# Scores of the last two cross-attentions from fp32r parts, with shared key places, keys' weights streamed in quarters, and values one step further ahead

## The reference

```python
def _cross_attention(q_in, kv_in, wq, bq, wk, bk, wv, bv, wo, bo, bias_k, bias_v):
    qh = (q_in @ wq + bq).reshape(b, q_len, H, K)
    kh = (kv_in @ wk + bk).reshape(b, t, H, K)
    vh = (kv_in @ wv + bv).reshape(b, t, H, K)
    kh = jnp.concatenate([kh, jnp.broadcast_to(bias_k, (b, 1, H, K))], axis=1)
    vh = jnp.concatenate([vh, jnp.broadcast_to(bias_v, (b, 1, H, K))], axis=1)
    logits = jnp.einsum('bqhk,bthk->bhqt', qh, kh) / jnp.sqrt(K)
    ctx = jnp.einsum('bhqt,bthk->bqhk', jax.nn.softmax(logits), vh).reshape(b, q_len, H * K)
    return ctx @ wo + bo
# x = x + attention 1(layer_norm(x)); x = x + attention 2(layer_norm(x)); x = x + mlp(layer_norm(x))
```

## Time and profile before

| | before |
|---|---|
| median of 3 runs | 1069.7 us (1068.66 to 1070.24) |
| the profiled execution, its own time | 1069.85 us |
| its span in the trace | 1068.0 us |
| PE, PEld busy share of the span | 94%, 74% |
| DVE, ACT, POOL busy share | 61%, 48%, 38% |
| mean granted TensorE clock | 0.992 |

### The profile page before, as it was taken

One profiled execution on the slowest core, in us unless ns is written; L12 is line 12 of the kernel. 1 busy time (PEld: TensorE's weight loads), 2 busy tenths in 40 slices (PEclk: granted clock), 3 DMA queues, 4 the chain that ended last, 5 costly groups with the idle time before them and its releaser, 6 DMA issues.

```text
span 1068.0 us, 18116 instructions
## 1 busy us (share of the span) xinstructions
PE 1006.1 (94%) x7252; PEld 789.6 (74%) x7252; DVE 656.5 (61%) x1119; ACT 512.2 (48%) x1026; POOL 402.8 (38%) x424
## 2 busy tenths in 40 slices
PE   6999999997998899999999999999999999989997
PEld 3667566555665898986777778777777877769997
DVE  4658999896787588355445436855434554554552
ACT  2557888876775554334333323323332332335552
POOL 2535689898876233002122113232211212443110
PEclk9999999999999899999999999999999999999999
DMA  9102000000000700020000114100000000200000
GB/s 322 61 1 80 1 1 1 2 1 2 2 1 2 256 2 2 1 79 1 2 1 1 29 52 158 56 24 1 1 1 1 2 1 1 79 1 12 20 21 30
DMA packets 17463, 34.90 MB, mean 33 GB/s; under 512 B 3554, under 2 KB 8420, under 8 KB 16740
## 3 DMA queue, kind: packets, MB, share of 16 engines
q1 hardware_dynamic: 17380, 33.75, 9.3%
HBM read 31.65 MB, written 2.10 MB: 32 GB/s over the span
## 4 chain that ended last, share of the span: by engine, by line
PE 74%; POOL 10%; ACT 6%; DVE 5%; issue 4%; DMA 0%; SPq 0%; POOLq 0%; DVEq 0%
PE work L938 11%; PE work L815 10%; PE scores L874 10%; PE work L891 5%; PE work L927 4%; POOL pair L1972 3%; PE work L674 3%; PE work L675 3%; PE work L676 3%; PE scores L674 3%; PE scores L676 3%; PE scores L675 3%; PE work L539 2%; PE work L601 2%; PE work L909 2%
## 5 line engine op out<-in xcount | busy, mean ns | idle before, releaser
L938 PE MATMUL work<-pair,probsT 128*128 128x256 f32 x512 | 120.5, 389 | 11.1 <-ACT pair L1845 8.9
L1931 POOL TENSOR_SCALAR stat<-stat 128x2 f32<-128x2 f32 (+1 forms) x49 | 11.2, 228 | 301.5 <-DVE stat L1060 300.3
L938 PEld LDWEIGHTS work<-pair,probsT 128*128 128x128 f32 x512 | 95.8, 192 | 35.4 <-issue 20.4
L815 PE MATMUL work<-ctxT,w 128*128 128x128 f32 x992 | 116.1, 275 | 1.8 <-ACT pair L1845 1.1
L815 PEld LDWEIGHTS work<-ctxT,w 128*128 128x128 f32 x992 | 114.5, 192 | 3.0 <-ACT pair L1845 1.3
L874 PE MATMUL scores<-pair,act_bufs 128*128 128x512 f32 x256 | 115.2, 592 | 0.0
L1836 ACT ACTIVATE pair<-work 128x512 f32<-128x512 f32 x64 | 38.2, 598 | 160.2 <-PE work L891 160.2
L1826 ACT ACTIVATE kvT<-work,cols 128x128 f32<-128x128 f32 x120 | 34.3, 369 | 142.1 <-PE work L815 142.1
L2086 POOL TENSOR_TENSOR probs<-probs,smax 128x1024 f32<-128x1024 f32 x22 | 42.0, 1909 | 152.6 <-DVE smax L1459 152.6
L1439 DVE TENSOR_REDUCE smax<-scores 128x16 f32<-128x1024 f32 x32 | 39.2, 1225 | 79.6 <-PE scores L874 79.6
L874 PEld LDWEIGHTS scores<-pair,act_bufs 128*128 128x128 f32 x256 | 46.3, 190 | 46.0 <-issue 45.9
(11 more groups left out here) (190 smaller groups left out, 2548.9 us busy)
## 6 DMA issues: line engine op xcount, KB each, us to landing
w<-in_l_wk SPq DMA_DIRECT2D x8, 512.0 KB, 7.2
w<-in_l_wq SPq DMA_DIRECT2D x8, 512.0 KB, 7.7
w<-in_l_wo SPq DMA_DIRECT2D x8, 512.0 KB, 8.1
w<-in_l_wv SPq DMA_DIRECT2D x8, 512.0 KB, 5.6
x<-in_x SPq DMA_DIRECT2D x1, 2048.0 KB, 13.7
out<-x SPq DMA_DIRECT2D x8, 256.0 KB, 2.1
pair<-in_xT SPq DMA_DIRECT2D x1, 1536.0 KB, 7.9
pair<-in_l_fc SPq DMA_DIRECT2D x1, 1024.0 KB, 5.1
```

The costliest lines, as they stand in the source:

```text
L815: last = mm(bank[:, h * P:(h + 1) * P], w[:, c, (4 * g + h) * K3:(4 * g + h + 1) * K3], ctxT[:, c, p * P:(p + 1) * P], start=(c == 0), sto ...
L938: last = mm(step_banks(j + 1)[0][:, 0:D], probsT_bufs[j % 2][:, q, :], pv[n % 2][:, bb, q, :], start=(q == 0), stop=(q == GH // 2 - 1))
```

## The change

1. `tile_scores` computes with `products`: for each of four key groups and two halves of the contraction, three fp32r matmuls of 256 columns (24 for a tile, in place of 4 fp32 ones of 512 columns). The tokens are kept as a high and a low part: DVE's `tile_source` writes both from PSUM (one instruction before, two now). The key products too: ACT copies the high part out, and DVE subtracts it from PSUM for the low part (`key_low`, two instructions a step). Whoever waited for ACT's copy of a key product (`a_pk`) now waits for DVE's low part (`d_kl`).
2. The key products lie in ten places, each of one group and one batch of the pair, given out by a table (`places_of_keys`); room for two comes from the half of `w3_wk` that is no longer used: the keys' weights are loaded one group at a time for every pair of batches (32 loads of 512 KB, two slots, in place of 8).
3. Values are worked on three steps ahead, not two.
4. ACT runs a one-column Gelu and a one-column Exp ahead of the first use of each; `key_bias(0)` and `key_bias(1)` go ahead of the stage's loop.
5. The last MLP's parts move to other addresses, and the copy of its first weight waits for the last value projection in place of an output.

```diff
         def value_of(j):
-            return j + 2 if 0 <= j + 2 < 8 * PAIRS else None
+            return j + 3 if 0 <= j + 3 < 8 * PAIRS else None
...
             for g in range(4):
-                load_w3(1, g, "kqo")
-
+                if g < 2:
+                    load_keys(g)
+                load_w3(1, g, "qo")
+
+            e.wait_ge(pe_f1, 4 * B)
+            for g in range(2):
+                load_w3(1, g, "v")
+            for i in range(2, 4):
+                e.wait_ge(pe_kp, i - 1)
+                load_keys(i)
...
             def first_free(j):
 
                 e.wait_ge(d_mr, B)
-                e.wait_ge(a_pk, 2 * keys_before(j))
+                e.wait_ge(d_kl, 2 * keys_before(j))
...
-                for half in range(2):
+                for g in range(4):
+                    k = place_at[PLACES[n, g][bb]]
                     for c in range(DC):
-                        last = mm(sc[j % 2][:, half * BANK:(half + 1) * BANK],
-                                  fixed[j // 2 % 2][:, c, t * P:(t + 1) * P],
-                                  pk[n % 2][:, bb, c, half * BANK:(half + 1) * BANK], start=(c == 0), stop=(c == DC - 1))
+                        last = products(sc[j % 2][:, g * QUARTER:(g + 1) * QUARTER],
+                                        [v[:, c, t * P:(t + 1) * P] for v in src_l3[j // 2 % 2]],
+                                        [all_keys[:, k + part, c, :] for part in range(2)], c == 0, c == DC - 1)
...
                     if q == 0:
                         third_free(j)
-                        e.wait_ge(a_pk, 2 * keys_before(j + 1) - 1)
+                        e.wait_ge(d_kl, 2 * keys_before(j + 1) - 1)
...
+            def key_low(i):
+
+                for c in range(DC):
+                    e.wait_ge(a_pk, 2 * i + c + 1)
+                    v.tensor_tensor(both_keys(i, c, 1), step_banks(i - 4)[2 + c][:, :].rearrange("p (h b k) -> p b h k", h=4, b=2),
+                                    both_keys(i, c, 0).bitcast(F32), ALU.subtract).then_inc(d_kl, 1)
...
+                if tile_of(j) is not None:
+                    tile_max_over(j)
+                if key_of(j) is not None:
+                    key_low(key_of(j))
                 if tile_of(j) is not None:
                     tile_shifted(j)
...
+            act(scratch[:, :], tanh_gate[:, :], ACT.Gelu_apprx_tanh)
...
+            key_bias(0)
+            key_bias(1)
+            act(scratch[:, :], tanh_gate[:, :], ACT.Exp)
             for j in STEPS:
                 key, value = key_of(j), value_of(j)
                 if key is not None:
-                    key_bias(key)
+                    if key >= 2:
+                        key_bias(key)
                     key_products(key)
```

More of the change, by code:

```diff
@@ L128, in build @@
         tanh_gate = sb("tanh_gate", [P, 1])
+        scratch = sb("scratch", [P, 1])
         probs_late = sb("probs_late", [P, GS + H3])
@@ L212, in parts_at @@
                     for i, k in enumerate(("high", "low"))]
+        src_l3 = [[nc.alloc_sbuf_tensor_at(f"src_l3_{i}_{k}", [P, DC, T], F32R, offset=at + 4 * i * DC * T)[:, :, :]
+                   for k, at in (("high", act_at), ("low", pair_at[1] + 4 * 2 * (n_kq + n_vo)))] for i in range(2)]
+        KEY_PLACES = 10
+        QUARTER = GS // 4
+        keys_at = w3_at + 4 * WN
+        all_keys = nc.alloc_sbuf_tensor_at("all_keys", [P, (pair_at[1] - keys_at) // 4 + n_kq * 2], F32R, offset=keys_at)
+        all_keys = all_keys[:, :].rearrange("p (k c n) -> p k c n", c=DC, n=QUARTER)
+        place_at = [(at - keys_at) // (4 * DC * QUARTER) + 2 * k for at, n in ((keys_at, 2), (pair_at[0], 4), (pair_at[1], 4))
+                    for k in range(n)]
+        assert len(place_at) == KEY_PLACES
         n_w, n_src, n_hid = 4 * DC * F, 4 * DC * T, 4 * FC * T
@@ L250, in build @@
         names += [f"l{i}_w{k}" for i in range(3) for k in "qkvo"]
-        names += [f"l3_w{k}_{g}" for k in "qkvo" for g in range(4)]
+        names += [f"l3_w{k}_{g}" for k in "qvo" for g in range(4)] + ["l3_wk_0", "l3_wk_1"]
         s_in = {n: sem(f"in_{n}") for n in names}
@@ L342, in key_bank, with places_of_keys, both_keys @@
             return fbank[i] if i < 2 else step_banks(i - 4)[0]
+        def places_of_keys():
+            places, used_until = {}, [-4 * PAIRS] * KEY_PLACES
+            for i in range(8 * PAIRS):
+                n, g = divmod(i, 4)
+                both = sorted(sorted(range(KEY_PLACES), key=lambda k: used_until[k])[:2])
+                assert max(used_until[k] for k in both) <= i - 4
+                places[n, g] = *both, max(0, *(used_until[k] + 1 for k in both))
+                for bb, k in enumerate(both):
+                    used_until[k] = 4 * n + 2 * bb + 1
+            return places
+        PLACES = places_of_keys()
+        def both_keys(i, c, part):
+            first, second, _ = PLACES[divmod(i, 4)]
+            a, b = place_at[first] + part, place_at[second] + part
+            return all_keys[:, a:b + 1:b - a, c, :].rearrange("p b (h k) -> p b h k", h=4)
         def attention_of(i):
@@ L409, in load_w3, with load_keys @@
                 heads, ks = slice(4 * g, 4 * g + 4), slice(4 * g * K3, (4 * g + 4) * K3)
[L410 to L412 removed]
+                for k in which:
                     src = A[f"l3_w{k}{a}"]
[L414 to L419 removed]
+                    if k == "v":
+                        load(f"l3_wv_{g}", w3_wv[:, g, :, :], src.rearrange("p (c n) -> p c n", c=DC)[:, :, ks])
+                    else:
+                        dst = w3_wq if k == "q" else w3_wo
+                        load(f"l3_w{k}_{g}", dst[:, heads, :], src.rearrange("p (h d) -> p h d", h=H3)[:, heads, :])
+            def load_keys(i):
+                a, _, g = attention_of(i)
+                load(f"l3_wk_{i % 2}", w3_wk[:, i % 2, :, :],
+                     A[f"l3_wk{a}"].rearrange("p (c n) -> p c n", c=DC)[:, :, 4 * g * K3:(4 * g + 4) * K3])
             e.wait_ge(d_res, NU)
```

83 lines of the change are left out of this document (48 added, 35 removed).

## The result

| | before | the change |
|---|---|---|
| median (lowest to highest), us | 1069.37 (1068.66 to 1070.24), 4 runs | 1051.65 (1050.85 to 1052.58), 4 runs |
| span of the profiled execution, us | 1068.0 | 1048.9 |
| steps 0 to 28, from scores to scores, us | 434.0 | 412.2 |

The ratio is 0.9834 (95% interval 0.9817 to 0.9851): 17.7 us faster.

A forecast was written before the change was run, and what follows sets the result against it. PE was taken to bound the kernel, busy for 94% of the span. From 1069.85 us, -15.4 - 8.2 - 1.7 - 1.1 + 0.6 + 2.0 + 5.9 + 3.4 = -14.5 gave 1055.3, or 1055.2 for the median; range 1046 to 1064.

The forecast's parts named there:

- Scores, -15.4: Score blocks: 24 fp32r matmuls take 2.96 us in place of 3.44, saving 0.48 on each of 32 tiles, 15.4 us less.
- Values three ahead, -8.2: Output matmuls: all 8.9 us of waits for ACT's value copies go, a 0.7 us tail wait comes; 8.2 us less.
- Clock in the tail, -1.7: Tail: with 0.7 us idle in place of 2.35, PE keeps full clock at the output; 1.7 us less.
- Tables, -1.1: Exp's table load leaves ACT's way to the first value copies, Gelu's move saves nothing; 1.1 us less.
- Steps 13 and 14, +2.0: DVE, also preparing the second attention, is late: PE waits about 1.4 us, then some 0.6 in the next step; +2.0.
- Lead-in, +5.9: Before the first scores: PE waits for DVE's low parts behind the value sums; 5.9 us more, without the moved value.
- Clock in the lead-in, +3.4: Lead-in: idle gaps of 2.4 and 2.6 us each bring the lower clock at 1.7 us; 3.4 us more.
- The tail at nothing: Tail: probabilities are ready 8.0 us after their scores, PE has 8.3 us of work in between; no cost.
- A: The lead-in costs less, as the clock holds and half of the gaps close: 1044 to 1050 us; chance 0.20.
- B: Low parts leak in every step: each of 28 steps with a key pays 0.3, 1060 to 1067 us; chance 0.17.
- C: POOL slows DVE's low parts from 0.69 to 1.28 us in steps with a key: slower, 1076 us; chance 0.05.
- D: Score blocks gain nothing from fp32r: 256-column matmuls issue at 0.143 us or more, time 1070; chance 0.03.

The follow-up runs named there:

- the fp32 run: The changed kernel with score products in fp32 of the high parts alone, low parts still made but left out of the scores: 1071.53 us.
- the run without preloads: The changed kernel without the two one-element activations that load the Gelu and Exp tables ahead: 1051.93 us.
- the turned order: The changed kernel with DVE making the keys' low parts ahead of the value sums in the four steps before the first scores: 1050.63 us.
- the run of the tail's order: The changed kernel with the mixing matrix's high and low parts for the last steps made earlier on ACT and POOL: 1048.29 us.

## Why the prediction was right

The forecast was 1055.2 for 1051.65, with the sign and the bound right, and most of the places. That the sum is only 3.6 us off is in part luck: against the measured parts it was too high by 9.2 us (scores 4.4, clock in the lead-in 3.4, lead-in 0.9, steps 13 and 14 0.5) and too low by 4.1 (tail 3.0, tables 1.1). Its steps:

- **Scores, -15.4.** The mechanism was right and the size too small: 32 x 0.62 = 19.8. The block is 2.91 and not 2.96, and the projections ahead of it lost 0.09, which I had not counted; the fp32 run gives it back, so it is of the scores. The trace still speaks against the 0.109 us of the Trainium skill (VectorE: DVE Perf Modes, engine table): a product costs 0.118.
- **Values three ahead, -8.2.** In the steps the seven waits are gone, 6.6 us, and the tail's 2.35 became 0.74, as said. But the price of leaving it out is 21 us, not 8, and the old kernel gains 6.0 from it. The term was right for the sum and says nothing about the parts: alone, values give -6.0, fp32r scores with their low parts and the rest give +4.1, both together -17.7. Low parts delay ACT's copies by 1.1 us, under seven outputs that waited for them already, so the third part is what lets the first one pay.
- **Clock in the tail, -1.7.** Right: no lower clock from 930 to 945.
- **Tables, -1.1.** Wrong; measured 0. The step that failed is "Exp's load lies on ACT's way to the first value copies". PE still waits 1.16 us there, for DVE's shift is now the later one. I moved DVE by 1.7 us in one term and did not ask what it did to this one. The Trainium skill's drain of 1.38 us (ScalarE: Activation LUTs, "What ACT_TABLE_LOAD costs") is not seen either: in the changed kernel ACT goes on 0.01 us after the load.
- **Step 0, +0.6.** Right: 0.61 waited, and 0.1 more.
- **Steps 13 and 14, +2.0.** Step 13 as worked out (1.39 for 1.4); in step 14 nothing, since DVE had caught up there: +1.5.
- **Lead-in, +5.9.** (Its working gives 9.5 - 3.66 = 5.8.) Measured +5.0, with waits of 2.11, 2.10, 1.65 and 1.64 for 2.4, 2.6, 1.9 and 1.9.
- **Clock in the lead-in, +3.4.** Wrong, 0 in the profiled execution, which shows full clock through both gaps. The step that failed is that a gap of the 2.35 us kind brings the lower clock for certain: in this lead-in it came in seven of the thirteen traces of changed kernels and experiments. (The change's other three executions have a mean clock of 0.993 against 0.995 and spans 0.7 to 1.2 us longer; no trace says where.) Nor would it have cost 3.4. In the run without preloads it did come:
```profile
462.00:464.00 2.00, 2.00 (x16) 2.00 (x15) 0.85 (x5) 0.00 (x0) 0.94 (x2) 0.74 0.37 141
464.00:466.00 2.00, 2.00 (x11) 2.00 (x11) 1.93 (x5) 0.14 (x1) 0.00 (x0) 0.50 0.00 0
```
(us, busy times, then the granted clock, DMA share and GB/s). Its key products took 3.12 us in place of 1.95, and the wait behind them was 0.52 in place of 2.10, since DVE is the pace there and does not slow down. Its lead-in is 43.97 against 43.90. In the turned order, where it fell on value products with no long wait behind them, it cost 1.6 (43.7 in three runs against 42.1 in one).
- **The tail at nothing.** Wrong by 3.0 us: "a tile's probabilities are ready 8.0 us after its scores, and PE has 8.3" was drawn from a normal step, in which POOL rests while DVE works on the maxima. PE's 8.3 was right for tile 29, but its probabilities took 9.8, and 7.8 in the run of the tail's order. Late probabilities are not the scores' doing alone: with values three ahead the kernel before waits 1.5 us for them too.
- **Other edits at nothing** holds: 0.02 us a step for low parts, places and streaming together.

Of the rivals, A's time was nearly reached, by another way than it said: no gap closed, the clock held and the scores gave more. B is excluded by the slack of 0.2 us. C's mechanism exists, in the tail and at DVE operations from SBUF, not where it was put: the keys' low parts never ran beside POOL and kept 0.69, and the tokens' low parts, which read PSUM and SBUF as they do, kept 0.69 the four times that they ran beside it. D fell with the first block of scores.

## What to carry to other kernels

When one edit makes the bounding engine faster and another makes its helpers later, price each edit with the other in place: here the scores without the values lose 4.1 us, and both together win 1.7%. A term that costs an operation's removal has to be read again after every other term that moves its neighbour on the same chain. And what a lower clock costs depends on what stands behind it: 0.07 us here where the next wait took it up, 1.6 us where none did.

## What the runs showed of the hardware

**The same wait may or may not lower the clock.** The last MLP's wait of 2.36 us stands in both these kernels. PE's timeline, first of the changed kernel, then of the one with the tail's order:
```profile
1038.33 0.55 PE L725 MATMUL work<-w_high,hid_high 128*128 128x256 f32 x1 [2.36 <-ACT hid_high L1966]
1038.67 0.41 PE L726 MATMUL work<-w_low,hid_high 128*128 128x256 f32 x1
```
```profile
1037.59 0.35 PE L725 MATMUL work<-w_high,hid_high 128*128 128x256 f32 x1 [2.36 <-ACT hid_high L1966]
1037.79 0.28 PE L726 MATMUL work<-w_low,hid_high 128*128 128x256 f32 x1
```
In one the granted clock of the window from 1038 to 1040 is 0.50, the lower level of 1.2 GHz, and products start 0.21 us apart; in the other it is 1.00, and they start 0.12 apart. Ten of the fourteen traces are like the first, four like the second, and the last MLP takes 109.3 to 109.5 us in the ten and 108.0 in the four. A wait of 1.7 to 1.8 us near 427 was followed by 0.50 in six of the twelve traces of changed kernels and experiments that have it, and by full clock in the change itself; it put PE 1.5 us back in the run of the tail's order. I found nothing in the program that tells these cases apart. So a term for the clock behind a gap of 1.7 to 2.4 us should be a chance, not a number.

**Some of DVE's operations from SBUF stand still beside POOL's two-input ones.** The 16-column operations took 0.59 and 1.28 us in place of 0.17 while POOL ran subtractions of 1.24 us each. The layer norm's last step (L1118, 256 columns) took 1.99 us the 14 times that it ran beside POOL's scaling of probabilities, and 0.41 alone. The maximum and the shift, which read PSUM, kept their 1.22 us, but so did the statistics (L1108) their 0.41, which read SBUF. SBUF — State Buffer of the Trainium skill ("SBUF: two separate sides") describes an exclusive lock on a port pair that DVE and GpSimd share, under which the loser waits for the whole instruction; on DVE's side it names operations in a two-port mode or with two SBUF inputs. The stretch of 1.11 us, nearly one POOL operation, agrees with it; which mode these operations run in, no run here shows.
